# Moving the end of batch 14 to GpSimd, and x, bias and beta behind the last projection

## The chip, the cores and the metric

The kernel runs on one core of one Trainium2 chip. The metric is the device time of one execution in microseconds (us). Execution times of the same kernel are compared as medians of runs. The engines are named as in the profile: PE (TensorE, the matmuls), PEld (its weight loads), DVE (VectorE), ACT (ScalarE), POOL (GpSimd), SP (SyncE, which here only issues DMAs); "q" behind a name (SPq) is the sequencer that issues for that engine.

## The reference

One conditioned transformer attention layer on x of 16 batches x 256 tokens x 256 channels, 16 heads. The feed-forward weights W1 and W2 are passed in and not used.

```python
def _sln(h, w, ln_g, ln_b, Wg, bg, Wb, bb):
    mu = jnp.mean(h, axis=-1, keepdims=True)
    var = jnp.mean((h - mu) ** 2, axis=-1, keepdims=True)
    ln = (h - mu) / jnp.sqrt(var + EPS) * ln_g + ln_b
    gamma = (w @ Wg.T + bg)[:, None, :]
    beta = (w @ Wb.T + bb)[:, None, :]
    return gamma * ln + beta
...
h = _sln(hidden, w, ln_g, ln_b, Wg, bg, Wb, bb)
qkv = (h @ Wqkv.T + bqkv).reshape(B, N, num_heads, hd, 3)
...
energy = jnp.einsum('bhqd,bhkd->bhqk', q, k)
att = jax.nn.softmax(energy, axis=-1) / D ** 0.5
out = jnp.einsum('bhqk,bhkd->bhqd', att, v)
...
out = out @ Wp.T + bp
h1 = out + hidden
h2 = _sln(h1, w, ln_g, ln_b, Wg, bg, Wb, bb)
return h2 + h1
```

## The kernel before, in words

The kernel works through the 16 batches one after another, software-pipelined: while the scores, the exponentials and the weighing of batch b run, the maxima of batch b + 1, the projections of batch b + 2 and the first layer norm of batch b + 3 are made, and the second layer norm of batch b - 2 ends. Each engine has its own program, written out by hand in order; every dependence between engines is a wait on a semaphore, and an engine that waits holds all that stands behind it in its program. A batch's 256 tokens lie as two halves (t = 0, 1) of 128 partitions x 256 channels.

What the change touches is the tail behind the loop over the batches. There the last two batches are finished: batch 14 (B - 2) and batch 15 (B - 1).

The second layer norm of a batch has these steps, with a the batch (function `residual`, DVE): the residual h1 = m1 + x (stage 0, L784), its statistics (`bn_stats`, stage 1), mean and variance mv2 (`bn_aggr`, stage 2, after a short `memset` of `pause`), vare = variance + EPS (stage 3, L799), then y = (h1 - mean) * gamma (stage 4, L804, two instructions) and y = y * rstd + h1b (stage 5, L812, two instructions). POOL makes h1b = h1 + beta (`add_beta`, L396) and rstd = vare ** -0.5 (`rstd_out`, L403) between them. gamma and beta of a batch lie in `gb` (columns 0 to D, and D to 2D). vare, rstd, mv2, h1 and h1b of the second norm have a single buffer, y has two (batch parity). `ln2_step` counts the DVE steps of this norm, `rstd_ready` the powers on POOL, `y_ready` the finished batches.

In batch 15 the last half of the attention is projected twice by PE in `finish`: into the banks st0 and st1 (`project_half(k, 0)`, `projt_done`), where x and bias have been added by a matmul with the identity, for the statistics (L948) and for (h1 - mean) * gamma (L956); and into m1 (`project_half(k, 1)`, `projb_done`), where x, bias and beta are added in the same way. The sum x + bias + beta is made by POOL into the tile xn (L491, `xb2_ready`). Both wait for aT_l, the low half of the attention output turned round, which DVE makes in two pieces (`low_att_half`, L833) from what ACT evicted (L677). The last two DVE instructions (L963, `yt_ready`) make y = y * rstd + m1, one for each half.

SP issues the result transfers in this order: batch 14 whole, 256 KB, after `y_ready` reaches B - 1 (L348), then the two halves of batch 15, 128 KB each, after `yt_ready` (L351), and waits for all of them to land (L353).

Of the kernel before, what the change touches and what calls it, by code (L numbers as in the profile page):

```python
# [32 lines left out]
P = 128  # L33
# [24 lines left out]
def cond_block(nc, x, condT, vectors, WgT, WbT, WqkvT, WpT, bp, out):  # L58
    gb_dram = nc.dram_tensor("gb_rows", (B, 2 * D), F32, kind="Internal").ap()
    with ExitStack() as ctx:  # L60
# [165 lines left out]
        h1b_ready = sem("h1b_ready")  # L226
        y_ready = sem("y_ready")

        def wait(eng, s, value):
# [20 lines left out]
        def par(a):  # L250

            return a % 2
# [103 lines left out]
        def _(pool):  # L356
# [116 lines left out]
            for k in range(KT):  # L473
# [13 lines left out]
            add_beta(B - 2)  # L487
            rstd_out(B - 2)
            wait(pool, gb_in[par(B - 1)], 16 * (half(B - 1) + 1))
            wait(pool, xdb_ready, B)  # L490
            pool.tensor_tensor(xn[:], xbuf(B - 1), gb[:, par(B - 1), D:2 * D].rearrange("p (a n) -> p a n", a=1)  # L491
                               .broadcast_to([P, TT, D]), ALU.add).then_inc(xb2_ready, 1)
            rstd_out(B - 1)

# [185 lines left out]
        def _(dve):  # L680
# [261 lines left out]
            low_att_half(0)  # L942
            residual(B - 2, 4)
            low_att_half(1)
            residual(B - 2, 5)
            for t in range(TT):
                wait(dve, projt_done, t + 1)
                o = dve.bn_stats(stats2[:, t, :], st_ps[t][:, 0:D])  # L948
            o.then_inc(ln2_step, 1)
            residual(B - 1, 2)  # L950
            residual(B - 1, 3)
            a = B - 1
# [5 lines left out]
            o.then_inc(ln2_step, 1)  # L958
            wait(dve, ln2_step, 4 * a + 4)
            wait(dve, rstd_ready, 1 * a + 6)  # L960
# [6 lines left out]
        def _(pe):  # L967
# [237 lines left out]
            def project_half(k, into):  # L1205

                for t in range(TT):
                    l = (aT_h[:, k, t * P:(t + 1) * P], aT_l[:, k, t * P:(t + 1) * P])
                    ps = st_ps[t][:, 0:D] if into == 0 else m1[:, t * D:(t + 1) * D]
                    for n, (a, w) in enumerate(((l[0], wp_h), (l[1], wp_h), (l[0], wp_l))):  # L1210
                        o = mm(ps, a, w[:, k, :], False, k == KT - 1 and n == 2 and (into == 0 or t == TT - 1))
                    if k == KT - 1 and into == 0:
                        o.then_inc(projt_done, 1)
                if k == KT - 1 and into == 1:
                    o.then_inc(projb_done, 1)

            def finish():
# [20 lines left out]
                project_half(1, 0)  # L1238
                wait(pe, h1_ready, B - 1)
                pe.wait_ge(xb2_ready, 1)  # L1240
                for t in range(TT):
                    mm(m1[:, t * D:(t + 1) * D], ident[:], xn[:, t, :], t == 0, False)
                for k in range(KT):
                    project_half(k, 1)

# [131 lines left out]
```

## Time and profile before

| what | before |
|---|---|
| time, median of 3 runs | 350.76 us |
| the 3 runs | 350.86, 348.23, 350.76 us |
| the profiled execution, its own time | 349.5 us |
| its span, first to last instruction | 347.7 us |
| granted TensorE clock, mean over the span | 0.99 |
| PE busy | 334.0 us (96%) |
| PEld busy | 288.6 us (83%) |
| DVE busy | 297.0 us (85%) |
| ACT busy | 242.8 us (70%) |
| POOL busy | 159.0 us (46%) |
| chain that ended last, by engine | PE 86%, DVE 5%, ACT 2%, DMA 2%, POOL 2%, issue 2% |

The profile is one execution, and its own time is 1.8 us above its span. Busy time is the sum of an engine's instructions; the chain that ended last is followed back from the last instruction through what released each step. Times in the trace are counted from the start of the span, so the tail that the change touches lies between about 334 and 344 us.

### The profile page before, as it was taken

The page shows a single profiled execution, that of the slowest core. Times are in us where ns is not written, and L with a number is a line of the kernel's source. Part 1 is how long each engine was busy: PE and PEld are TensorE (multiplying, and loading weights), DVE is VectorE, ACT ScalarE, POOL GpSimd, SP SyncE. Part 2 cuts the span into 40 slices and gives each one's busy share as a digit, 9 for nine tenths or more (in the row PEclk, how much of TensorE's full clock was granted, in tenths as well). Part 3 has the DMA queues.
Part 4 walks back from the last instruction along what each step waited for, and adds up shares of the span by engine and source line. Part 5 has one row for each costly group of instructions (what it writes and reads, how often), then busy time and mean ns, then how long its engine had stood idle before and what let it go on. Part 6 is the DMA issues. An engine that isn't in the chain of part 4 may idle for free.

```text
span 347.7 us, 8982 instructions
## 1 busy us (share of the span) xinstructions
PE 334.0 (96%) x3173; PEld 288.6 (83%) x3173; DVE 297.0 (85%) x728; ACT 242.8 (70%) x476; POOL 159.0 (46%) x187
## 2 busy tenths in 40 slices
PE   8886989999999999999999999999999999999993
PEld 4675968889898888888898888888898888888773
DVE  4874877789898989989898989989898988998684
ACT  7762686868678686868687686868687686766740
POOL 5476261525464462726454462726454453225330
PEclk9997899999999999999999999999999999999999
DMA  8487245544555465565545565656546454652011
GB/s 239 128 202 204 58 123 151 150 134 129 161 131 158 135 180 155 136 173 139 157 133 156 134 176 153 141 154 160 156 135 154 106 170 124 168 147 75 18 60 60
DMA packets 47705, 48.87 MB, mean 141 GB/s; under 512 B 6287, under 2 KB 41374, under 8 KB 47662
## 3 DMA queue, kind: packets, MB, share of 16 engines
q1 hardware_dynamic: 44782, 47.00, 49.3%
q0 software_dynamic: 1984, 0.51, 0.9%
q10 hardware_dynamic: 896, 0.80, 0.8%
q8 instruction: 25, 0.41, 0.5%
q14 instruction: 18, 0.15, 0.1%
HBM read 9.99 MB, written 4.23 MB: 41 GB/s over the span
## 4 chain that ended last, share of the span: by engine, by line
PE 86%; DVE 5%; ACT 2%; DMA 2%; POOL 2%; issue 2%; SPq 0%; DVEq 0%; POOLq 0%; ACTq 0%
PE m L969 24%; PE st L969 19%; PE sa L969 18%; PE pv L969 17%; PE pv L1058 4%; PE pv L1139 2%; PE m L1098 2%; DMA wqkv<-WqkvT_dram 2%; DVE mx L688 1%; DVE qk_l L723 1%; POOL qk_l L415 1%; POOL xn L378 1%; PE pv L1072 1%; PE m L1072 1%; ACT qk_h L522 0%
## 5 line engine op out<-in xcount | busy, mean ns | idle before, releaser
L688 DVE TENSOR_REDUCE mx<-sa 128x2 f32<-128x512 f32 x256 | 171.6, 683 | 30.1 <-PE sa L969 29.0
L602 ACT ACTIVATE p<-st 128x512 f32<-128x512 f32 x240 | 140.9, 598 | 38.0 <-PE st L969 33.9
L969 PE MATMUL sa<-kst,qst 126*128 126x256 f32 x512 | 106.5, 290 | 1.6 <-DVE mx L688 1.1
L969 PE MATMUL st<-qst,kst 128*128 128x256 f32 x496 | 104.0, 292 | 0.7 <-DMA qst<-m_l 0.5
L969 PEld LDWEIGHTS st<-qst,kst 128*128 128x128 f32 x496 | 75.1, 188 | 14.3 <-issue 12.8
L969 PEld LDWEIGHTS sa<-kst,qst 126*128 126x128 f32 x512 | 80.0, 193 | 3.8 <-DVE mx L688 2.1
L369 POOL DMA_DIRECT2D qst<-m_h x31 | 17.6, 566 | 117.0 <-DVE m_l L697 117.0
L969 PE MATMUL pv<-p,v_st 128*32 128x256 f32 x1008 | 61.0, 382 | 0.0
L969 PEld LDWEIGHTS pv<-p,v_st 128*32 128x32 f32 x1008 | 29.5, 109 | 21.0 <-ACT p L602 1.8
L969 PE MATMUL m<-hT_h,wqkv_h 128*128 128x256 f32 x128 | 36.8, 300 | 1.4 <-issue 0.8
L378 POOL TENSOR_SCALAR xn<-xa,mv,rstd 128x256 f32<-128x256 f32 x28 | 34.2, 1227 | 1.4
L969 PE MATMUL m<-hT_h,wqkv_l 128*128 128x256 f32 x128 | 34.4, 280 | 0.4 <-DVE wqkv_l L909 0.4
L969 PE MATMUL m<-hT_l,wqkv_h 128*128 128x256 f32 x128 | 34.2, 279 | 0.0
L430 POOL TENSOR_TENSOR rstd<-vare,minus_half 128x4 f32<-128x4 f32 (+1 forms) x15 | 14.2, 947 | 40.4 <-DVE vare L745 36.3
L550 ACT ACTIVATE oT<-pv 128x512 f32<-128x512 f32 x29 | 17.2, 594 | 21.6 <-PE pv L969 21.6
L723 DVE SCALAR_TENSOR_TENSOR qk_l<-m,vecs,qk_h 128x256 fp32r<-128x256 f32 x60 | 25.9, 473 | 0.6 <-ACT qk_h L522 0.6
L969 PEld LDWEIGHTS m<-hT_h,wqkv_h 128*128 128x128 f32 x128 | 23.5, 189 | 2.3 <-ACT wqkv_h L642 1.2
L969 PEld LDWEIGHTS m<-hT_h,wqkv_l 128*128 128x128 f32 x128 | 23.6, 190 | 0.6 <-DVE wqkv_l L909 0.6
L969 PEld LDWEIGHTS m<-hT_l,wqkv_h 128*128 128x128 f32 x128 | 23.4, 187 | 0.0
L396 POOL TENSOR_TENSOR h1b<-h,gb 128x512 f32<-128x512 f32 x15 | 19.3, 1289 | 6.9 <-DVE h L784 6.9
L387 POOL TENSOR_TENSOR xa<-xa,bias_b 128x512 f32<-128x512 f32 x16 | 20.6, 1292 | 0.0
L410 POOL TENSOR_TENSOR hT_l<-hT,hT_h 128x512 fp32r<-128x512 f32 x14 | 18.0, 1289 | 4.0 <-ACT hT_h L503 4.0
(149 smaller groups left out, 568.3 us busy)
## 6 DMA issues: line engine op xcount, KB each, us to landing
qst<-qk_h SPq DMA_DIRECT2D x64, 128.0 KB, 2.4
qst<-qk_l SPq DMA_DIRECT2D x64, 128.0 KB, 2.5
kst<-qk_l SPq DMA_DIRECT2D x64, 128.0 KB, 2.7
kst<-qk_h SPq DMA_DIRECT2D x62, 128.0 KB, 2.4
xa<-x_dram SPq DMA_DIRECT2D x16, 256.0 KB, 3.0
gb<-gb_rows SPq DMA_DIRECT2D x16, 256.0 KB, 3.9
out_dram<-y SPq DMA_DIRECT2D x15, 256.0 KB, 3.4
wqkv<-WqkvT_dram SPq DMA_DIRECT2D x1, 512.0 KB, 5.8
```

The costliest lines, as they stand in the source:

```text
L369: pool.dma_start(raw(qst[MAX_ROW + r:MAX_ROW + 1 + r, p, g * HH:(g + 1) * HH, :]) .rearrange("a h (t n) -> a (h t) n", t=TT), raw(m[:, g, ...
L378: o = pool.tensor_scalar(xn[:, t, :], xbuf(a)[:, t, :], mv[:, t, 0:1], rstd[:, 0, t:t + 1], ALU.subtract, ALU.mult)
L387: pool.tensor_tensor(xbuf(a), xbuf(a), bias_b[:].rearrange("p (a n) -> p a n", a=1).broadcast_to([P, TT, D]), ALU.add).then_inc(xdb_ready, 1)
L396: pool.tensor_tensor(h1b[:], h1[:], gb[:, par(a), D:2 * D].rearrange("p (a n) -> p a n", a=1) .broadcast_to([P, TT, D]), ALU.add).then_inc ...
L410: pool.tensor_tensor(hT_l[:, par(a)], hT[:], hT_h[:, par(a)], ALU.subtract).then_inc(hTl_ready, 1)
L430: pool.tensor_tensor(rstd[:, which], vare[:, which], minus_half[:, which], ALU.pow).then_inc(rstd_ready, 1)
L550: nc.scalar.activation(oT[:, g, :], pv_ps[g][:], ACT.Copy).then_inc(oT_ready, 1)
L602: nc.scalar.activation(p32[:, h, :], st_ps[h % 2][:], ACT.Exp).then_inc(exp_done, 1)
L688: dve.tensor_reduce(mx[:, par(a), h // HH, (h % HH) * TT:(h % HH + 1) * TT], sa_ps[h % 2][:].rearrange("p (t n) -> p t n", t=TT), AX.X, AL ...
L723: o = dve.scalar_tensor_tensor(out=qk_l[:, par(a), t, g, :], in0=ps[:, g * N:(g + 1) * N], scalar=vecs[:, 4 + t, g:g + 1], in1=qk_h[:, par ...
L969: return nc.tensor.matmul(o, l, r, start=start, stop=stop)
L1058: o = nc.tensor.transpose(pv_ps[g][:, t * N + c * P:t * N + (c + 1) * P], oT[:, g, c * N + t * P:c * N + (t + 1) * P], ident[:])
```

## The change

Batch 14's last two steps leave DVE: the four instructions of stages 4 and 5 are gone from its program. POOL makes them in other pieces: right behind rstd of batch 14 two `tensor_scalar` make (h1 - mean) * rstd; then comes, as before, x + bias + beta for batch 15; then a `tensor_tensor` multiplies by gamma; then rstd of batch 15; then a `tensor_tensor` adds h1b and counts `y_ready`. A new semaphore `xhat_ready` orders these steps, and DVE waits until it is 2 before it overwrites mv2 with batch 15's values. The calls `residual(B - 1, 2)` and `residual(B - 1, 3)` are written out, since the count of `ln2_step` is one lower. On PE the two matmuls that add x, bias and beta into m1 stand behind the twelve of the projection instead of ahead of them. SP's program is the same.

```diff
--- before.py
+++ after.py
@@ -225,6 +225,7 @@
         ln2_step = sem("ln2_step")
         h1b_ready = sem("h1b_ready")
         y_ready = sem("y_ready")
+        xhat_ready = sem("xhat_ready")
 
         def wait(eng, s, value):
 
@@ -486,11 +487,24 @@
             add_beta(B - 3)
             add_beta(B - 2)
             rstd_out(B - 2)
+            a = B - 2
+            wait(pool, y_out[par(a)], 16 * half(a))
+            wait(pool, rstd_ready, 1 * a + 6)
+            for t in range(TT):
+                pool.tensor_scalar(y[:, par(a), t, :], h1[:, t, :], mv2[:, t, 0:1], rstd[:, 1, t:t + 1],
+                                   ALU.subtract, ALU.mult).then_inc(xhat_ready, 1)
             wait(pool, gb_in[par(B - 1)], 16 * (half(B - 1) + 1))
             wait(pool, xdb_ready, B)
             pool.tensor_tensor(xn[:], xbuf(B - 1), gb[:, par(B - 1), D:2 * D].rearrange("p (a n) -> p a n", a=1)
                                .broadcast_to([P, TT, D]), ALU.add).then_inc(xb2_ready, 1)
-            rstd_out(B - 1)
+            pool.wait_ge(xhat_ready, 2)
+            pool.tensor_tensor(y[:, par(a)], y[:, par(a)], gb[:, par(a), 0:D].rearrange("p (a n) -> p a n", a=1)
+                               .broadcast_to([P, TT, D]), ALU.mult).then_inc(xhat_ready, 1)
+            wait(pool, ln2_step, 4 * (B - 1) + 2)
+            pool.tensor_tensor(rstd[:, 1], vare[:, 1], minus_half[:, 1], ALU.pow).then_inc(rstd_ready, 1)
+            wait(pool, h1b_ready, B - 1)
+            pool.wait_ge(xhat_ready, 3)
+            pool.tensor_tensor(y[:, par(a)], y[:, par(a)], h1b[:], ALU.add).then_inc(y_ready, 1)
 
         @block.scalar
         def _(act):
@@ -940,15 +954,19 @@
             normalise_half(0)
             normalise_half(1)
             low_att_half(0)
-            residual(B - 2, 4)
             low_att_half(1)
-            residual(B - 2, 5)
             for t in range(TT):
                 wait(dve, projt_done, t + 1)
                 o = dve.bn_stats(stats2[:, t, :], st_ps[t][:, 0:D])
             o.then_inc(ln2_step, 1)
-            residual(B - 1, 2)
-            residual(B - 1, 3)
+            dve.wait_ge(xhat_ready, 2)
+            wait(dve, ln2_step, 4 * (B - 1))
+            dve.memset(pause[:], 0.0)
+            for t in range(TT):
+                o = dve.bn_aggr(mv2[:, t, :], stats2[:, t, :])
+            o.then_inc(ln2_step, 1)
+            wait(dve, ln2_step, 4 * (B - 1) + 1)
+            dve.tensor_scalar(vare[:, 1], mv2[:, :, 1], EPS, None, ALU.add).then_inc(ln2_step, 1)
             a = B - 1
             wait(dve, y_out[par(a)], 16 * half(a))
             wait(dve, gb_in[par(a)], 16 * (half(a) + 1))
@@ -956,7 +974,7 @@
                 o = dve.scalar_tensor_tensor(out=y[:, par(a), t, :], in0=st_ps[t][:, 0:D], scalar=mv2[:, t, 0:1],
                                              in1=gb[:, par(a), 0:D], op0=ALU.subtract, op1=ALU.mult)
             o.then_inc(ln2_step, 1)
-            wait(dve, ln2_step, 4 * a + 4)
+            wait(dve, ln2_step, 4 * a + 3)
             wait(dve, rstd_ready, 1 * a + 6)
             dve.wait_ge(projb_done, 1)
             for t in range(TT):
@@ -1208,11 +1226,10 @@
                     l = (aT_h[:, k, t * P:(t + 1) * P], aT_l[:, k, t * P:(t + 1) * P])
                     ps = st_ps[t][:, 0:D] if into == 0 else m1[:, t * D:(t + 1) * D]
                     for n, (a, w) in enumerate(((l[0], wp_h), (l[1], wp_h), (l[0], wp_l))):
-                        o = mm(ps, a, w[:, k, :], False, k == KT - 1 and n == 2 and (into == 0 or t == TT - 1))
+                        o = mm(ps, a, w[:, k, :], into == 1 and k == 0 and t == 0 and n == 0,
+                               into == 0 and k == KT - 1 and n == 2)
                     if k == KT - 1 and into == 0:
                         o.then_inc(projt_done, 1)
-                if k == KT - 1 and into == 1:
-                    o.then_inc(projb_done, 1)
 
             def finish():
                 wait(pe, att_ready, 2 * B - 1)
@@ -1237,11 +1254,12 @@
                 pe.wait_ge(aTtl_ready, 2)
                 project_half(1, 0)
                 wait(pe, h1_ready, B - 1)
+                for k in range(KT):
+                    project_half(k, 1)
                 pe.wait_ge(xb2_ready, 1)
                 for t in range(TT):
-                    mm(m1[:, t * D:(t + 1) * D], ident[:], xn[:, t, :], t == 0, False)
-                for k in range(KT):
-                    project_half(k, 1)
+                    o = mm(m1[:, t * D:(t + 1) * D], ident[:], xn[:, t, :], False, t == TT - 1)
+                o.then_inc(projb_done, 1)
 
             def step(b):
                 for h in range(H):
```

The end of DVE's program before, from the last normalise of the attention's second half. A row is a line, an operation and what it writes from what; `sa`, `pv`, `st` and `m` are banks of PSUM, `h` is h1, `mv` is mv2, `stats` is stats2:

```order
L833 TENSOR_TENSOR aT_l<-sa,aT_h 128x256 [waits aTth_ready]
L804 SCALAR_TENSOR_TENSOR y<-h,mv,gb 128x256 [waits gb_in0,y_out0]
L804 SCALAR_TENSOR_TENSOR y<-h,mv,gb 128x256
L833 TENSOR_TENSOR aT_l<-pv,aT_h 128x256 [waits aTth_ready]
L812 SCALAR_TENSOR_TENSOR y<-y,rstd,h1b 128x256 [waits h1b_ready,rstd_ready,ln2_step]
L812 SCALAR_TENSOR_TENSOR y<-y,rstd,h1b 128x256
L948 BN_STATS stats<-st 128x6 [waits projt_done] x2
L793 MEMSET pause 128x1 [waits ln2_step]
L795 BN_AGGR mv<-stats 128x2 x2
L799 TENSOR_SCALAR vare<-mv 128x2 [waits ln2_step]
```

The same place of the changed kernel (its lines are 14 to 18 higher):

```order
L847 TENSOR_TENSOR aT_l<-sa,aT_h 128x256 [waits aTth_ready]
L847 TENSOR_TENSOR aT_l<-pv,aT_h 128x256 [waits aTth_ready]
L960 BN_STATS stats<-st 128x6 [waits projt_done] x2
L964 MEMSET pause 128x1 [waits ln2_step,xhat_ready]
L966 BN_AGGR mv<-stats 128x2 x2
L969 TENSOR_SCALAR vare<-mv 128x2 [waits ln2_step]
L974 SCALAR_TENSOR_TENSOR y<-st,mv,gb 128x256 [waits gb_in1,y_out1]
L974 SCALAR_TENSOR_TENSOR y<-st,mv,gb 128x256
L981 SCALAR_TENSOR_TENSOR y<-y,rstd,m 128x256 [waits projb_done,rstd_ready,ln2_step]
```

The two pairs of batch 14 are out; the two halves of aT_l stand next to each other, and the `memset` has a second wait. What follows `vare` is as before.

The end of POOL's program before:

```order
L396 TENSOR_TENSOR h1b<-h,gb 128x512 [waits y_ready,h1_ready,gb_in0]
L403 TENSOR_TENSOR rstd<-vare,minus_half 128x2 [waits y_ready,ln2_step]
L491 TENSOR_TENSOR xn<-xa,gb 128x512 [waits xdb_ready,gb_in1]
L403 TENSOR_TENSOR rstd<-vare,minus_half 128x2 [waits y_ready,ln2_step]
```

And of the changed kernel:

```order
L397 TENSOR_TENSOR h1b<-h,gb 128x512 [waits y_ready,h1_ready,gb_in0]
L404 TENSOR_TENSOR rstd<-vare,minus_half 128x2 [waits y_ready,ln2_step]
L494 TENSOR_SCALAR y<-h,mv,rstd 128x256 [waits rstd_ready,y_out0]
L494 TENSOR_SCALAR y<-h,mv,rstd 128x256
L498 TENSOR_TENSOR xn<-xa,gb 128x512 [waits xdb_ready,gb_in1]
L501 TENSOR_TENSOR y<-y,gb 128x512 [waits xhat_ready]
L504 TENSOR_TENSOR rstd<-vare,minus_half 128x2 [waits ln2_step]
L507 TENSOR_TENSOR y<-y,h1b 128x512 [waits xhat_ready,h1b_ready]
```

Two instructions now stand ahead of the one that makes xn, one more ahead of rstd of batch 15, and one behind it, which releases batch 14's transfer.

## Rows read from the trace of the kernel before

**Rows 1.** The chain that ended last, its end: start us, us, what.

```profile
337.80 0.41 DVE aT_l L833
338.22 0.68 DVE y L804 x2
338.89 0.22 issue
339.12 0.42 DVE aT_l L833
339.58 0.97 PE st L969 x6
340.56 2.24 PE m L969 x16
...
342.92 0.48 DVE y L963
```

**Rows 2.** Timeline of ACT: start us, us, engine, line, operation, [idle before].

```profile
338.41 0.38 ACT L677 ACTIVATE aT_h<-pv 128x256 fp32r<-128x256 f32 x1 [1.33 <-PE pv L1233]
```

**Rows 3.** Timeline of PE, the last of st, the identity matmuls, the last of m.

```profile
340.28 0.28 PE L969 MATMUL st<-wp_l,aT_h 128*128 128x256 f32 x1
340.39 1.03 PE L969 MATMUL m<-xn,ident 128*128 128x256 f32 x4
...
342.51 0.28 PE L969 MATMUL m<-wp_l,aT_h 128*128 128x256 f32 x1
```

**Rows 4.** Timeline of DVE in the tail.

```profile
340.24 0.79 DVE L948 BATCH_NORM_STATS2 stats<-st 128x6 f32<-128x256 f32 x2
...
341.35 0.17 DVE L799 TENSOR_SCALAR vare<-mv 128x2 f32<-128x2 f32 x1
341.43 0.88 DVE L956 SCALAR_TENSOR_TENSOR y<-st,mv,gb 128x256 f32<-128x256 f32 x2
342.92 0.87 DVE L963 SCALAR_TENSOR_TENSOR y<-y,rstd,m 128x256 f32<-128x256 f32 x2 [0.62 <-PE m L969]
```

**Rows 5.** Timeline of POOL in the tail.

```profile
334.85 1.29 POOL L396 TENSOR_TENSOR h1b<-h,gb 128x512 f32<-128x512 f32 x1 [6.89 <-DVE h L784]
336.57 0.71 POOL L403 TENSOR_TENSOR rstd<-vare,minus_half 128x2 f32<-128x2 f32 x1 [0.43 <-DVE vare L799]
337.24 1.27 POOL L491 TENSOR_TENSOR xn<-xa,gb 128x512 f32<-128x512 f32 x1
341.59 0.71 POOL L403 TENSOR_TENSOR rstd<-vare,minus_half 128x2 f32<-128x2 f32 x1 [3.08 <-DVE vare L799]
```

**Rows 6.** Timeline of SP's transfers, of batch 14 and of batch 15.

```profile
340.34 0.34 SPq L348 DMA_DIRECT2D out_dram<-y  x1
343.43 0.81 SPq L351 DMA_DIRECT2D out_dram<-y  x2
```

**Rows 7.** Instructions on tile y from 338 to 346 us, and SP's last wait.

```profile
L804 DVE SCALAR_TENSOR_TENSOR y<-h,mv,gb x2: 473/568/664, 338.1 to 338.7; 128x256 f32<-128x256 f32 x2
L351 SPq DMA_DIRECT2D out_dram<-y x2: 337/380/422, 343.4 to 343.8; - x2
DMA to landing us min/median/max: 1.7/1.8/2.0
...
L353 SPq EVENT_SEMAPHORE  x1: 17/17/17, 345.6 to 345.6; - x1
```

**Rows 8.** Groups of POOL instructions, each shape apart: count | busy us, mean ns | idle.

```profile
L378 POOL TENSOR_SCALAR xn<-xa,mv,rstd 128x256 f32<-128x256 f32 x28 | 34.2, 1227 | 1.4
L387 POOL TENSOR_TENSOR xa<-xa,bias_b 128x512 f32<-128x512 f32 x16 | 20.6, 1292 | 0.0
...
L474 POOL TENSOR_SCALAR bias_cols<-ones,vecs 128x128 f32<-128x128 f32 x2 | 0.7, 369 | 0.2
```

**Rows 9.** Line L378 alone: duration ns min/median/max.

```profile
L378 POOL TENSOR_SCALAR xn<-xa,mv,rstd x28: 1209/1228/1232, 26.4 to 277.1; 128x256 f32<-128x256 f32 x28
```

**Rows 10.** Timeline of POOL in the loop: a power, then the tensor_scalar pair.

```profile
79.71 1.03 POOL L430 TENSOR_TENSOR rstd<-vare,minus_half 128x4 f32<-128x4 f32 x1 [2.98 <-DVE vare L745]
80.85 2.44 POOL L378 TENSOR_SCALAR xn<-xa,mv,rstd 128x256 f32<-128x256 f32 x2
```

**Rows 11.** Line L745 in two stretches, and POOL beside its second start.

```profile
L745 DVE TENSOR_SCALAR vare<-mv x1: 168/168/168, 4.6 to 4.6; 128x2 f32<-128x2 f32 x1
...
L745 DVE TENSOR_SCALAR vare<-mv x2: 169/363/557, 13.0 to 17.2; 128x2 f32<-128x2 f32 x2
...
16.24 3.81 POOL L458 MEMSET kst<- 128x512 f32 x8 [2.22 <-DVE xn L750]
```

**Rows 12.** Groups of DVE instructions: the add that POOL's is compared with.

```profile
L784 DVE TENSOR_TENSOR h<-m,xa 128x512 f32<-128x512 f32 x15 | 10.1, 671 | 1.0 <-PE m L969 1.0
```

**Rows 13.** Transfers between 325 and 348 us: GB/s in 40 slices.

```profile
GB/s 0 10 19 0 0 0 0 0 28 0 0 0 0 0 0 221 310 157 75 146 4 0 0 0 0 0 0 0 324 132 0 0 0 157 276 23 0 0 0 0
```

## The prediction, on record before the changed kernel ran

> **What bounds the kernel now.** Over its whole span PE is the bound, but nothing that the change touches lies ahead of 337 us, so I read only the end. I went to the chain that ended last, from its end backwards [rows 1]: the last DVE instruction waits for PE's projection into m1, PE's projection waits for the second aT_l of DVE (339.12), and that aT_l stood behind two y instructions of batch 14 (338.22, 0.68 us). The timeline of ACT [rows 2] shows what that place cost: ACT had finished the input of that aT_l at 338.41 + 0.38 = 338.79, and DVE began at 339.12. So 0.3 us of the chain is DVE's work for batch 14, sitting in the way of batch 15. Behind it the chain is PE alone until 342.79 [rows 3], then L963 at 342.92 [rows 4], then two issues of SP from 343.43 to 344.24, SP's wait until the landing at 345.6, and the close of the program [rows 6, 7].
>
> Two things in these views matter as much as the chain. POOL idles 3.08 us ahead of the rstd of batch 15 [rows 5]: that is the room the change wants to fill. And SP issues batch 14 at 340.34, right after DVE's L812, 3.1 us ahead of the first half of batch 15 [rows 6]: today the order "14, then 15" on SP's queue costs nothing, because 14 is long done.
>
> **The change part by part.**
>
> *DVE loses four instructions.* The second aT_l can start at 338.79 + 0.04 (the step between two engines in the chain is 0.02 to 0.05 us) = 338.83 in place of 339.12: 0.3 us earlier. PE's six matmuls into st then start at 339.28 instead of 339.58, the second bn_stats follows 0.3 us earlier too, since it began at 340.60, just behind PE's last st matmul (340.28 + 0.28 = 340.56) [rows 3, 4]; so vare of batch 15 moves from 341.35 to 341.05, and L956's pair from 341.43 to 341.13. The new wait of the memset for xhat_ready = 2 asks for 339.8 (below) and is met a microsecond ahead.
>
> *PE's order.* The same twelve matmuls into m1 and the same two identity matmuls (four records, 1.03 us) in another order: no cost by itself. What it buys is cover: xn is needed at 341.5 in place of 340.1. Before, from the start of st to the end of m PE took 342.79 - 339.58 = 3.21 us; now it ends at 339.28 + 3.21 = 342.5, if xn is there when PE has done the twelve, at about 341.5. Had the order stayed, PE would have waited for xn until 341.0.
>
> *POOL gains four instructions.* I follow its queue by start times, with its own rows for each kind. Neighbouring POOL instructions overlap by 0.04 us (336.57 + 0.71 against 337.24) [rows 5]; one that waits for the one before it starts 0.1 us after its end (79.71 + 1.03 = 80.74 against 80.85) [rows 10].
> - rstd of batch 14 ends at 336.57 + 0.71 = 337.28, unchanged.
> - Two tensor_scalar with two per-partition scalars, 128x256: the same form as L378, 28 times in the trace, 1.209 to 1.232 us each with DVE busy beside it [rows 9]; 2.43 us a pair, from 337.38 to 339.81.
> - xn, 1.27 us [rows 5]: from 339.77 to 341.04. PE has it 0.4 us before it wants it.
> - The multiply by gamma, 128x512 from two SBUF tiles. No multiply of this form is in the trace. Nearest is the add of the same shape, 1.27 to 1.29 us [rows 5, 8]. Bounds: not below 0.74 (two of L474's 0.369 for 128 columns, which does two operations but reads one tensor [rows 8]), not above the 2.45 of two L378. I take the add, since only the operation differs: 341.00 to 342.29.
> - rstd of batch 15: now 342.25 to 342.96, where before it ran 341.59 to 342.30. DVE's last pair waits for it and can start at 343.00 instead of 342.92. The whole gain of the first step is eaten here, and 0.08 us more.
> - The add of h1b, 1.29 us [rows 5]: 342.92 to 344.21. Only this counts y_ready.
>
> *SP's queue.* Here the end is set. Batch 14's transfer stands ahead of batch 15's on SP, and it is now released at 344.21, not at 340.31. It issues at 344.24, takes 0.34 us and a gap of 0.04, and the two halves follow in 0.81 us: the last issue ends at 344.24 + 0.38 + 0.81 = 345.43, where it ended at 344.24 [rows 6]. That is **+1.2 us**. The rows of batch 15, ready at 343.48 and 343.87, wait for nothing but SP's order.
>
> *The transfers themselves.* 512 KB now leave in one piece where 256 KB did. Landing took 2.0 us for the whole batch and 1.7 to 1.8 for a half [rows 7]. Unhindered the last half lands 1.8 us behind its issue at 345.02, at 346.82. If instead it queues: batch 14 lands at 346.24, and the other 256 KB at the best rate of a slice, 324 GB/s [rows 13], take 0.8 us more: 347.05. So 0 to +0.25 us; I take +0.1, since a half takes nearly as long to land as a whole (1.8 against 2.0), so size is the small part of it.
>
> Sum: 1.2 + 0.1 = **+1.3 us** on the profiled execution: span 347.7 + 1.3 = 349.0, time 349.5 + 1.3 = 350.8.
>
> The profiled 349.5 lies inside the three runs (348.23, 350.76, 350.86), whose median is 350.76. With the median as base the sum gives 352.1, with the profiled run 350.8. These runs lie wider apart than the effect, so I take a value between: **351.5 us**.
>
> A row and a rule on moving elementwise work. An add of 128x512 takes DVE 0.671 us [rows 12] and POOL 1.29 [rows 8], a ratio of 1.92; and the new POOL work is 2.45 + 1.29 + 1.29 = 5.0 us against the 0.87 x 2 DVE spends. The Trainium skill, GPSIMD Engine Reference, section 3.1, has POOL 1.96 times slower at an add of 2048 fp32 elements and says that "use DVE for elementwise" stays the rule. The trace agrees on the ratio for an add; by the rule's ratio alone the moved 1.74 us would be 3.4 us and POOL would be done 1.6 us sooner, at 342.6, so the rule's direction is right and its size too kind for this form.
>
> **The rivals.**
>
> *A. vare held up by POOL.* vare of batch 15 wants to start at 341.05, 0.05 us after POOL's multiply. The trace shows a DVE instruction of this very form held: L745 took 0.557 us at 17.2 in place of 0.168, while POOL ran back-to-back memsets of 0.48 us [rows 11]; and the first L804 took 0.664 in place of 0.473, begun while POOL's xn was running [rows 5, 7]. If vare is held to the end of the multiply, it ends at about 342.35, the power starts at 342.4 instead of 342.25, and all behind it is 0.15 us later; L974's pair ends at 343.25, DVE's last pair at 344.1, still ahead of SP. Total +1.45: 352.9 on the median base, 351.65 by my middle value. Against it: the start times are equal within their error, so vare may slip in first.
> The Trainium skill, SBUF — State Buffer, section "Who interferes with whom", says that a DVE instruction in a 2-port mode (tensor_scalar can be one) and a POOL instruction exclude each other for a whole instruction. Both rows above agree that DVE is held; by it rival A would be the rule whenever the multiply starts first.
>
> *B. The multiply is dear.* At its upper bound, 2.45, rstd of batch 15 and the last add move 1.16 us: +2.5 in all, 352.7. For it: no multiply row; against it: its neighbours differ by 0.02.
>
> *C. Hidden or faster.* POOL's chain ends early enough that SP issues 14 before 15 is ready. Then PE's 0.3 us gain shows: -0.3, 349.9. It needs y_ready by about 342.6, that is 1.6 us off the 5.0 of new POOL work. If the two tensor_scalar cost as L474 does (0.74 each) it saves only 1.0: y_ready 343.23, last issue ends 343.26 + 0.38 + 0.81 = 344.45, +0.2. The 28 rows of L378 speak against even that.
>
> *D. Slower by over 1%.* POOL's new instructions stretched because both engines work on the same memory in turn. To pass 3.5 us, the 5.0 us must grow by 3.5 - 1.3 = 2.2 us, 44%; at twice the length it is +5.0 + 1.3 = +6.3, 357. Against it: L378's 28 durations lie within 2% beside a busy DVE [rows 9], and DVE's instructions here mostly read PSUM.
>
> **How the numbers follow.** Forecast as summed (POOL's chain and SP's order, +1.0 to +1.35): 0.47. A: 0.30. B: 0.12. C: 0.07. D: 0.04. All but D lie within 1%, about what a measurement of this kernel can tell from no change (350.76 +/- 3.5). Chances: faster by over 1% 0.01, within 1% 0.95, slower by over 1% 0.04. Range: below, the forecast on the lowest run, 348.23 + 1.3 = 349.5, and C just under it; above, B on the median base, 350.76 + 2.5 = 353.3. I give 349.2 to 353.3.
>
> **What would show each step.** In the profile after: the second aT_l on DVE near 338.85 and PE's first st matmul 0.3 us sooner than before; POOL without a gap from 336.6 to 344.2, with 1.23 us for each new tensor_scalar and 1.29 for the multiply; rstd of batch 15 near 342.3, released not by DVE but by POOL's own queue; DVE's last pair waiting for rstd, not for PE; batch 14's transfer issued near 344.2 with both halves of batch 15 right behind it, and the last landing near 346.9. A is shown by vare of over 1 us. I am wrong if SP's three issues don't stand together at the end, or if y_ready falls before 343.

## The result, and the profile after

| what | before | changed |
|---|---|---|
| time, median (22 runs each) | 349.01 us (348.04 to 351.09) | 351.16 us (350.26 to 352.94) |
| ratio to before, 95% interval | | 1.0055 (1.0038 to 1.0072) |
| the profiled execution, its own time | 349.5 us | 351.13 us |
| its span | 347.7 us | 349.3 us |

The changed kernel is slower by 0.55%, 1.9 us (1.3 to 2.5), within the 1% called no change in the prediction but clear of zero; the two medians lie 2.15 us apart. One of the 12 executions of a_no_mul, below, was a slow one of 817 us, and its ratio leaves it out. In the page the busy times show little: POOL has 4 instructions and 6.3 us more (159.0 to 165.3), DVE 4 instructions less.

```profile
span 349.3 us, 8981 instructions
PE 334.0 (96%) x3173; PEld 288.6 (83%) x3173; DVE 296.6 (85%) x724; ACT 242.5 (69%) x476; POOL 165.3 (47%) x191
```

The tail of the changed kernel, timeline of POOL (start us, us, engine, line, operation), which answers to [rows 5]:

```profile
336.06 0.71 POOL L404 TENSOR_TENSOR rstd<-vare,minus_half 128x2 f32<-128x2 f32 x1 [0.44 <-DVE vare L813]
336.95 2.44 POOL L494 TENSOR_SCALAR y<-h,mv,rstd 128x256 f32<-128x256 f32 x2 [0.18 <-POOL rstd L404]
339.36 1.30 POOL L498 TENSOR_TENSOR xn<-xa,gb 128x512 f32<-128x512 f32 x1
340.62 1.28 POOL L501 TENSOR_TENSOR y<-y,gb 128x512 f32<-128x512 f32 x1
341.99 0.72 POOL L504 TENSOR_TENSOR rstd<-vare,minus_half 128x2 f32<-128x2 f32 x1
342.68 1.27 POOL L507 TENSOR_TENSOR y<-y,h1b 128x512 f32<-128x512 f32 x1
```

Timeline of DVE, which answers to [rows 4]:

```profile
338.33 0.42 DVE L847 TENSOR_TENSOR aT_l<-pv,aT_h 128x256 fp32r<-128x256 f32 x1 [0.61 <-ACT aT_h L691]
339.47 0.78 DVE L960 BATCH_NORM_STATS2 stats<-st 128x6 f32<-128x256 f32 x2 [0.71 <-PE st L987]
...
340.67 1.24 DVE L969 TENSOR_SCALAR vare<-mv 128x2 f32<-128x2 f32 x1
341.83 0.86 DVE L974 SCALAR_TENSOR_TENSOR y<-st,mv,gb 128x256 f32<-128x256 f32 x2
342.80 0.87 DVE L981 SCALAR_TENSOR_TENSOR y<-y,rstd,m 128x256 f32<-128x256 f32 x2
```

Timeline of PE (its last rows) and of SP, which answer to [rows 3] and [rows 6]:

```profile
341.03 1.03 PE L987 MATMUL m<-xn,ident 128*128 128x256 f32 x4
...
343.97 0.34 SPq L349 DMA_DIRECT2D out_dram<-y  x1
344.35 0.93 SPq L352 DMA_DIRECT2D out_dram<-y  x2
```

The span starts of two executions are no good origin: the tail of this one began 0.5 us sooner than before's (rstd of batch 14 on POOL at 336.06 against 336.57 [rows 5]), in parts of the program that are alike. From here on, "at x" without more is counted in us from the start of that instruction, which nothing in any of these kernels touches. In this measure, before: POOL's last instruction ends at 5.73, SP's last issue at 7.67, the span at 11.13. Changed: 7.89, 9.22 and 13.24. So the tail is **2.1 us** longer, and the span shows 1.6 only because of the 0.5 ahead of it. The span and the rows of the programs' close are printed to 0.1 us, so sums that use them are good to about 0.05.

2.1 us is more than SP's issues are late (1.55) and more than the last landing is late: SP passes its last wait (taken here and below as the start of its first closing row, the COMPARE_BRANCH of line L60, whose rows follow under a_no_mul) at 9.13 before and at 10.74 after, 1.6. What lies between that wait and the end grew from 2.0 to 2.5 us, with nothing in the change that would explain it. That rest is what the experiments followed.

### The profile page after: what moved, and what is told of

Its sections match the earlier page's. It is cut to its first block, busy times and chain, and to the rows that moved or that the text cites. A ratio compares the mean times of both kernels' runs of the same rounds, so it can differ in the third digit from the quotient of the medians.

```text
span 349.3 us, 8981 instructions
## 1 busy us (share of the span) xinstructions
PE 334.0 (96%) x3173; PEld 288.6 (83%) x3173; DVE 296.6 (85%) x724; ACT 242.5 (69%) x476; POOL 165.3 (47%) x191
## 4 chain that ended last, share of the span: by engine, by line
PE 84%; DVE 5%; ACT 4%; POOL 3%; issue 2%; POOLq 0%; ACTq 0%; DVEq 0%
PE m L987 23%; PE st L987 18%; PE sa L987 18%; PE pv L987 17%; PE pv L1076 4%; PE pv L1157 2%; PE m L1116 2%; DVE mx L702 1%; ACT qst L620 1%; DVE qk_l L737 1%; POOL qk_l L416 1%; POOL xn L379 1%; PE pv L1090 1%; PE m L1090 1%; ACT qk_h L536 0%
```

## The experiments

Theory 1 is the prediction's: POOL's chain releases batch 14's transfer late, SP's order holds batch 15 behind it, and the last landing sets the end. The first four kernels test it.

**b_hold14**, before with batch 14's transfer held back until the first half of batch 15 is ready, so that SP's three issues stand together as in the changed kernel, and no compute touched:

```diff
+            sp.wait_ge(yt_ready, 1)
             wait(sp, y_ready, B - 1)
             sp.dma_start(out_t[B - 2], y[:, par(B - 2)]).then_inc(y_out[par(B - 2)], 16)
```

> The kernel before, with one wait more on SP: batch 14's transfer is issued only when the first half of batch 15 is ready (as in the changed kernel it stands directly ahead of the two halves); no compute engine is touched. Times counted from the start of the rstd of batch 14 on POOL: before, SP's last issue ends at 7.67 us, its last wait at 9.03, the span at 11.1; in the changed kernel 9.22, 10.74, 13.2. Theory 1 (SP's order and three transfers close together are a cost of their own): last issue ends at 8.05 (+0.38), last wait at 9.6 (+0.55), and if the longer close of the program (2.5 us in place of 2.1) comes from the three transfers too, the span ends at 12.1, +1.0; with a close of 2.1 it is +0.55. Rival (only POOL's chain costs, the transfers overlap freely): last wait +0.38 and close 2.1, +0.4 in all.

Measured: ratio to before 0.9997 (0.9973 to 1.0021). Its span is 347.6 us, and rstd of batch 14 starts at 336.50. Rows of SP and of the close:

```profile
343.74 0.93 SPq L352 DMA_DIRECT2D out_dram<-y  x2
...
L60 POOLq DRAIN  x1: 5892/5892/5892, 341.5 to 341.5; - x1
L60 SPq COMPARE_BRANCH  x1: 33/33/33, 346.2 to 346.2; - x1
```

SP's last issue ends at 8.17 (+0.5), its last wait at 9.70 (+0.57), as theory 1 said, and the span ends at 11.10: not a trace of it arrived at the end. Both theories on record were wrong here; the close shrank by what the landing was late, so the end hangs on something else.

**a_15first**, the changed kernel with batch 15's halves issued first:

```diff
-            wait(sp, y_ready, B - 1)
-            sp.dma_start(out_t[B - 2], y[:, par(B - 2)]).then_inc(y_out[par(B - 2)], 16)
             for t in range(TT):
                 sp.wait_ge(yt_ready, t + 1)
                 sp.dma_start(out_t[B - 1][:, t, :], y[:, par(B - 1), t, :]).then_inc(y_out[par(B - 1)], 16)
+            wait(sp, y_ready, B - 1)
+            sp.dma_start(out_t[B - 2], y[:, par(B - 2)]).then_inc(y_out[par(B - 2)], 16)
```

> The changed kernel with SP's last issues turned round: the two halves of batch 15 first, batch 14 behind them. Theory 1 (batch 14 ahead on SP's queue holds batch 15 back): the halves issue at 7.2 us from the start of rstd of batch 14 and end by 8.15, batch 14 issues at 8.2, last issue ends at 8.55 in place of 9.22, last landing at about 10.2 in place of 10.74; 0.5 to 0.7 us faster than the changed kernel, still 1.0 to 1.5 us slower than before. Rival (POOL's late end is all of it, order is nothing): no faster than the changed kernel.

Measured: 1.0049 (1.0029 to 1.0070). Its span is 349.0 us, and rstd of batch 14 starts at 335.69:

```profile
342.94 0.81 SPq L350 DMA_DIRECT2D out_dram<-y  x2
343.80 0.45 SPq L352 DMA_DIRECT2D out_dram<-y  x1
...
L60 SPq COMPARE_BRANCH  x1: 33/33/33, 346.0 to 346.0; - x1
```

SP's last issue ends at 8.56, its last wait at 10.31, both 0.4 to 0.7 sooner than in the changed kernel, and the span ends at 13.31 against 13.24. Again what SP gains is not seen.

**a_act_vare**, the changed kernel with vare of batch 15 made by ACT (`eps_col` is a column holding EPS):

```diff
+            wait(act, ln2_step, 4 * (B - 1) + 1)
+            nc.scalar.activation(vare[:, 1], mv2[:, :, 1], ACT.Identity, bias=eps_col[:]).then_inc(vare_act, 1)
...
-            dve.tensor_scalar(vare[:, 1], mv2[:, :, 1], EPS, None, ALU.add).then_inc(ln2_step, 1)
...
-            wait(pool, ln2_step, 4 * (B - 1) + 2)
+            pool.wait_ge(vare_act, 1)
```

> The changed kernel, but variance + EPS of batch 15 is made by ACT, which is idle there, in place of DVE. Theory (rival A of the prediction: vare, 1.24 us in place of 0.16, was held by POOL's multiply): ACT's instruction takes under 0.4 us although POOL's multiply runs, the subtract and multiply by gamma on DVE start 1.1 us earlier, POOL's power starts right behind its multiply, 0.13 us sooner (5.80 us from the start of rstd of batch 14 in place of 5.93), and all behind it the same 0.13. Rival (vare was late for another reason, such as the wait on xhat_ready): ACT's instruction is as late or as long.

Measured: 1.0078 (1.0050 to 1.0105), too wide to tell 0.16 us: it holds the changed kernel's 1.0055, and lies above it if anywhere. What follows is read from the traces alone. Its timelines of ACT, POOL and DVE:

```profile
341.28 0.30 ACT L697 ACTIVATE vare<-mv,eps_col 128x2 f32<-128x2 f32 x1 [2.43 <-DVE mv L973]
...
341.15 1.29 POOL L504 TENSOR_TENSOR y<-y,gb 128x512 f32<-128x512 f32 x1
342.39 0.72 POOL L507 TENSOR_TENSOR rstd<-vare,minus_half 128x2 f32<-128x2 f32 x1
...
341.22 0.88 DVE L980 SCALAR_TENSOR_TENSOR y<-st,mv,gb 128x256 f32<-128x256 f32 x2
```

ACT's instruction takes 0.30 us in the middle of POOL's multiply; on DVE the same addition of EPS, with the same multiply beside it, took 1.24 and ended at 340.67 + 1.24 = 341.91, the end of the multiply (340.62 + 1.28 = 341.90). The power starts at 5.77 in place of 5.93, and the end comes at 13.08 in place of 13.24. Rival A is shown in the traces, one of each kernel, with its price: 0.16 us.

**a_no_mul**, the changed kernel without POOL's multiply by gamma for batch 14, which is left out of the computation:

```diff
-            pool.wait_ge(xhat_ready, 2)
-            pool.tensor_tensor(y[:, par(a)], y[:, par(a)], gb[:, par(a), 0:D].rearrange("p (a n) -> p a n", a=1)
-                               .broadcast_to([P, TT, D]), ALU.mult).then_inc(xhat_ready, 1)
...
-            pool.wait_ge(xhat_ready, 3)
+            pool.wait_ge(xhat_ready, 2)
```

> The changed kernel without POOL's multiply by gamma for batch 14 (that part of the computation is left out). Theory (POOL's queue sets the end, SP's order passes it on): xn's add is followed by the power as soon as vare is there, vare takes 0.16 again, the add of h1b ends 1.1 us sooner, batch 14 issues at about 6.8 us from the start of rstd of batch 14 in place of 7.91, the last issue ends at 8.1 in place of 9.22: 1.1 us faster. Rival (PE or DVE bound the end by then): under 0.5 us faster.

Measured: 1.0027 (1.0002 to 1.0052); vare 0.17 us, SP's last issue at 8.14, the end at 12.22, 1.0 sooner than in the changed kernel. POOL's last instruction ends at 6.81, 1.08 sooner. SP moved by as much here, so this kernel alone doesn't part the two; but together with b_hold14 and a_15first it is the clue: the end follows POOL, whether SP moves or not. In the six traces at hand the span ends 5.35 to 5.42 us behind POOL's last instruction. The rows of line L60, where each engine's program closes, say why. Before and changed (start us behind the durations in ns):

```profile
L60 POOLq DRAIN  x1: 5892/5892/5892, 341.6 to 341.6; - x1
L60 DVEq DRAIN  x1: 853/853/853, 343.0 to 343.0; - x1
L60 SPq COMPARE_BRANCH  x1: 33/33/33, 345.7 to 345.7; - x1
L60 POOLq EVENT_SEMAPHORE  x2: 17/17/17, 347.5 to 347.6; - x2
L60 SPq EVENT_SEMAPHORE  x1: 17/17/17, 347.6 to 347.6; - x1
```

```profile
L60 POOLq DRAIN  x1: 7056/7056/7056, 342.0 to 342.0; - x1
L60 DVEq DRAIN  x1: 853/853/853, 342.9 to 342.9; - x1
L60 SPq COMPARE_BRANCH  x1: 33/33/33, 346.8 to 346.8; - x1
L60 POOLq EVENT_SEMAPHORE  x2: 17/17/17, 349.1 to 349.2; - x2
L60 SPq EVENT_SEMAPHORE  x1: 17/17/17, 349.3 to 349.3; - x1
```

POOL's queue closes with a DRAIN that ends at 341.6 + 5.9 = 347.5 before and at 342.0 + 7.1 = 349.1 in the changed kernel, 5.2 us behind POOL's last instruction in both, and all other engines pass their last semaphore right behind it. SP is through its wait for the landing 1.8 to 2.3 us earlier and only waits for POOL. The row of a DRAIN can start before the engine's last instruction, so what counts is where it ends: DVE's ends at 343.0 + 0.85, less than 0.1 us behind DVE's last instruction (343.79). This is **theory 2**: POOL's last instruction plus 5.4 us ends the program, unless SP's last wait, plus 0.4, is later.

**b_pool_late**, before with an add on POOL whose result is not used:

```diff
             rstd_out(B - 1)
+            pool.wait_ge(rstd_ready, B + 5)
+            pool.tensor_tensor(h1b[:], h1[:], gb[:, par(B - 2), D:2 * D].rearrange("p (a n) -> p a n", a=1)
+                               .broadcast_to([P, TT, D]), ALU.add)
```

> The kernel before with one add of 128x512 more on POOL behind its last power; nothing waits for it and its result is not used. The profiles so far show a DRAIN on POOL's queue that ends 5.2 us behind POOL's last instruction, and the span ends 0.2 us behind that: 5.35 to 5.4 us behind POOL's last instruction in each of six kernels. Theory 2 (that DRAIN ends the program): POOL's last instruction ends 7.0 us from the start of rstd of batch 14 in place of 5.7, the span ends at 12.4 in place of 11.1, +1.25 us, although SP's last wait stays at 9.0. Theory 1 (SP's transfers end it): no change.

Measured: 1.0065 (1.0039 to 1.0091). The timelines of POOL and SP, and the close:

```profile
341.90 1.27 POOL L495 TENSOR_TENSOR h1b<-h,gb 128x512 f32<-128x512 f32 x1
...
342.95 0.81 SPq L351 DMA_DIRECT2D out_dram<-y  x2
...
L353 SPq EVENT_SEMAPHORE  x1: 17/17/17, 345.2 to 345.2; - x1
...
L60 POOLq DRAIN  x1: 6436/6436/6436, 341.9 to 341.9; - x1
```

SP's last issue ends at 7.68 and its wait at 9.12, as before to 0.01 us, and the span ends at 12.42 in place of 11.13: +1.29, for an instruction that nobody waits for. Theory 1 gives nothing here. The ratio says more, 2.3 us (1.4 to 3.2): it bears out that the kernel is slower, the size of 1.29 is the trace's, and what lies between the two is not explained.

**b_act_root**, before with batch 15's 1/sqrt off POOL. The power on POOL goes; ACT and DVE have in its place:

```diff
+            nc.scalar.activation(spare[:], eps_col[:], ACT.Sqrt)
+            wait(act, ln2_step, 4 * (B - 1) + 2)
+            nc.scalar.activation(vare[:, 1], mv2[:, :, 1], ACT.Sqrt, bias=eps_col[:]).then_inc(root_ready, 1)
...
-            residual(B - 1, 3)
...
+            dve.wait_ge(root_ready, 1)
+            dve.reciprocal(rstd[:, 1], vare[:, 1]).then_inc(ln2_step, 1)
...
-            rstd_out(B - 1)
```

> The kernel before with batch 15's 1/sqrt(variance + EPS) off POOL: ACT makes the square root (with a first use of the function ahead of time, so that its table is there), DVE the reciprocal of 128x2. POOL's last instruction is then the add that makes xn, ending 1.95 us from the start of rstd of batch 14 in place of 5.7. Theory 2: POOL's DRAIN ends by 7.2, so SP's last wait at 9.0 sets the end, and the span ends at 9.4 in place of 11.1: 1.7 us faster than before. Theory 1 (SP's transfers and a fixed close of 2.1 us behind them): no change, 11.1.

Measured: 0.9957 (0.9933 to 0.9982), 1.5 us faster than before (0.6 to 2.3). Rows of its ACT, of SP and of its close:

```profile
340.17 1.28 ACT L682 ACT_TABLE_LOAD   x1
341.46 0.20 ACT L682 ACTIVATE spare<-eps_col 128x1 f32<-128x1 f32 x1
342.70 0.30 ACT L684 ACTIVATE vare<-mv,eps_col 128x2 f32<-128x2 f32 x1 [1.03 <-DVE mv L802]
...
344.81 0.81 SPq L355 DMA_DIRECT2D out_dram<-y  x2
...
L60 POOLq DRAIN  x1: 6819/6819/6819, 338.2 to 338.2; - x1
...
L60 SPq COMPARE_BRANCH  x1: 33/33/33, 347.1 to 347.1; - x1
```

POOL's DRAIN is over at 345.0, 2.1 us ahead of SP's wait, which now sets the end: 9.58, 1.55 sooner than before, although batch 15's results are issued no sooner (7.70). Faster than both kernels.

**b_best**, the same with two edits more:

```diff
-            residual(B - 2, 4)
-            low_att_half(1)
...
+            for t in range(TT):
+                o = dve.scalar_tensor_tensor(out=y[:, par(a), t, :], in0=h1[:, t, :], scalar=mv2[:, t, 0:1],
+                                             in1=gb[:, par(a), 0:D], op0=ALU.subtract, op1=ALU.mult)
+                if t == 0:
+                    low_att_half(1)
...
+            act.wait_ge(yt_ready, 2)
+            act.dma_start(out_t[B - 1][:, 1, :], y[:, par(B - 1), 1, :]).then_inc(y_out[par(B - 1)], 16)
```

> b_act_root, and two edits more: the second aT_l of DVE stands between the two halves of batch 14's subtract and multiply in place of behind both, and the second half of batch 15's result is issued by ACT's queue beside SP's. Theory 2: PE's last projections start 0.25 us sooner, the two halves issue at once (0.4 us), and with POOL's DRAIN long over both show: the span ends at 8.7 us from the start of rstd of batch 14, 2.4 us faster than before. Under theory 1 it would be 0.65 faster.

Measured: 0.9918 (0.9890 to 0.9946), median 346.75 us, 2.9 us faster than before by the ratio (1.9 to 3.8). In the trace the end is at 9.25, 1.9 sooner than before and 0.3 sooner than in b_act_root; 8.7 was expected. Timelines of SP, ACT and DVE:

```profile
342.17 0.34 SPq L354 DMA_DIRECT2D out_dram<-y  x1
...
342.57 0.38 ACTq L685 DMA_DIRECT2D out_dram<-y  x1
...
341.66 0.87 DVE L980 SCALAR_TENSOR_TENSOR y<-y,rstd,m 128x256 f32<-128x256 f32 x2 [0.18 <-PE m L986]
```

The 0.24 us of PE arrived (DVE's last pair at 6.11 in place of 6.35 [rows 4, 5]), but the second queue brought next to nothing: the second half is ready only at 342.53, when SP would have been free again. I had counted 0.4 us of issue time that lies behind DVE's own work.

The other four isolate parts of the change. **a_pe_old**, the changed kernel with PE's old order:

```diff
+                pe.wait_ge(xb2_ready, 1)
+                for t in range(TT):
+                    mm(m1[:, t * D:(t + 1) * D], ident[:], xn[:, t, :], t == 0, False)
                 for k in range(KT):
                     project_half(k, 1)
-                pe.wait_ge(xb2_ready, 1)
-                for t in range(TT):
-                    o = mm(m1[:, t * D:(t + 1) * D], ident[:], xn[:, t, :], False, t == TT - 1)
-                o.then_inc(projb_done, 1)
```

> The changed kernel with PE's old order: the identity matmuls that add x, bias and beta stand ahead of the twelve of the last projection. PE then waits for xn until 4.6 us from the start of rstd of batch 14, its projection ends 0.4 us later than in the changed kernel, and DVE's last pair starts at 7.15 in place of 6.74. POOL's last instruction stays at 7.9, so by theory 2 the end stays at 13.2; by theory 1 too, since batch 14's issue at 7.9 still goes first.

One execution. PE waits for xn, and DVE's last pair starts at 7.35, 0.6 later than in the changed kernel (0.4 expected), yet the end is at 13.24, the same:

```profile
341.66 1.10 PE L987 MATMUL m<-xn,ident 128*128 128x256 f32 x4 [0.98 <-POOL xn L498]
```

**b_pe_new**, before with the new order on PE alone (the same lines the other way round):

> The kernel before with the change's order on PE alone: x, bias and beta are added into m1 behind the twelve matmuls of the last projection. xn is there 2 us before either order wants it. PE's last projection ends where it did, within 0.1 us, and the span ends at 11.1 us from the start of rstd of batch 14, under both theories.

One execution: DVE's last pair at 6.42 in place of 6.35, the end at 11.12. By itself PE's reordering makes DVE's last pair 0.07 us later and moves the end by nothing; in the changed kernel it hides what POOL's xn is late.

**b_split**, before with the second aT_l between the two halves of batch 14's subtract and multiply (the first part of b_best's edit, alone):

> The kernel before with the second aT_l of DVE between the two halves of batch 14's subtract and multiply; nothing else. PE's last projection and DVE's last pair come 0.25 us sooner, SP's last wait at 8.8 us from the start of rstd of batch 14 in place of 9.05. Theory 2: the power on POOL stays where it was within 0.05 us, so the span ends at 11.1 as before: a step on the chain that the profile names is shortened and the end does not move. Theory 1: the end moves 0.25 us.

One execution: PE and DVE's last pair 0.27 sooner, SP's last wait at 8.84 (9.13 before), and the end at 11.34, 0.2 **later**. It was expected unchanged. The reason is in theory 2's own measure: POOL's power ends at 5.94 in place of 5.73, since vare comes later. Its rows of DVE (rstd of batch 14 starts at 335.26):

```profile
337.86 0.48 DVE L947 SCALAR_TENSOR_TENSOR y<-h,mv,gb 128x256 f32<-128x256 f32 x1
338.38 0.88 DVE L812 SCALAR_TENSOR_TENSOR y<-y,rstd,h1b 128x256 f32<-128x256 f32 x2
339.17 0.76 DVE L955 BATCH_NORM_STATS2 stats<-st 128x6 f32<-128x256 f32 x2
```

The same instructions stand ahead of bn_stats, but L812 now comes directly behind the instruction whose count it waits for, and starts 0.04 us after that one's end, where before the aT_l lay between and the starts overlapped; and the aT_l is started only when ACT is done. bn_stats starts at 3.91 in place of 3.67. The chain that the profile printed for before got shorter and the program longer.

**a_h1b_dve**, the changed kernel with the add of h1b given back to DVE:

```diff
-            wait(pool, h1b_ready, B - 1)
-            pool.wait_ge(xhat_ready, 3)
-            pool.tensor_tensor(y[:, par(a)], y[:, par(a)], h1b[:], ALU.add).then_inc(y_ready, 1)
...
+            wait(dve, h1b_ready, B - 1)
+            dve.wait_ge(xhat_ready, 3)
+            dve.tensor_tensor(y[:, par(B - 2)], y[:, par(B - 2)], h1b[:], ALU.add).then_inc(y_ready, 1)
```

> The changed kernel with its last POOL instruction, the add of h1b for batch 14, given back to DVE, ahead of DVE's last pair. Theory 2 (POOL's last instruction sets the end): POOL's last instruction is the power, ending 6.65 us from the start of rstd of batch 14 in place of 7.89; the span ends at 12.0 to 12.05 in place of 13.24, 1.2 us faster than the changed kernel and still 0.9 slower than before, although DVE's last pair starts 0.5 us later and its results with it. Theory 1: SP's last issue ends at 8.65 in place of 9.22, 0.6 faster than the changed kernel.

Measured: 1.0023 (0.9990 to 1.0055); DVE's last pair starts at 7.14, 0.4 later than in the changed kernel, POOL's last instruction ends at 6.64, and the end is at 12.06: 1.2 sooner. Its close:

```profile
L60 POOLq DRAIN  x1: 5902/5902/5902, 343.9 to 343.9; - x1
L60 SPq COMPARE_BRANCH  x1: 33/33/33, 348.1 to 348.1; - x1
```

All of them side by side. The first column is where rstd of batch 14 starts in the trace; the others are in us from there (worked out from the timelines, the L60 rows and the spans; the last column is the end less POOL's last end):

| kernel | rstd of batch 14 starts | POOL's last instruction ends | SP's last wait over | span ends | behind POOL |
|---|---|---|---|---|---|
| before | 336.57 | 5.73 | 9.13 | 11.13 | 5.40 |
| b_pe_new | 335.38 | 5.74 | 9.22 | 11.12 | 5.38 |
| b_hold14 | 336.50 | 5.73 | 9.70 | 11.10 | 5.37 |
| b_split | 335.26 | 5.94 | 8.84 | 11.34 | 5.40 |
| a_h1b_dve | 338.04 | 6.64 | 10.06 | 12.06 | 5.42 |
| a_no_mul | 337.78 | 6.81 | 9.72 | 12.22 | 5.41 |
| b_pool_late | 336.08 | 7.09 | 9.12 | 12.42 | 5.33 |
| a_act_vare | 336.62 | 7.73 | 10.58 | 13.08 | 5.35 |
| a_pe_old | 336.96 | 7.86 | 10.74 | 13.24 | 5.38 |
| changed | 336.06 | 7.89 | 10.74 | 13.24 | 5.35 |
| a_15first | 335.69 | 7.89 | 10.31 | 13.31 | 5.42 |
| b_act_root | 337.92 | 1.95 | 9.18 | 9.58 | 7.63 |
| b_best | 335.55 | 1.95 | 8.85 | 9.25 | 7.30 |

In eleven kernels the end is 5.33 to 5.42 behind POOL, whatever SP does between 8.84 and 10.74; in the two where POOL is done early it is 0.40 behind SP's last wait. The scatter of 0.1 us is no more than the rounding of the spans. The ratios of the changed kernel, a_15first, a_act_vare, a_no_mul, b_pool_late, b_act_root and b_best are clear of 1 on the side that the table has; that of a_h1b_dve holds 1. The order among the slower kernels is the traces' alone, one of each, and b_split, b_pe_new and a_pe_old were executed only once.

## Why the prediction was right in its number and wrong in its reason

- **DVE's gain**: right. The second aT_l starts 0.04 behind ACT (337.91 + 0.38, then 338.33), at 2.27 in place of 2.55, 0.28 sooner for the 0.29 forecast. vare started only 0.17 sooner (4.61 in place of 4.78), not 0.30: the memset, which now has two waits, began 0.14 behind bn_stats in place of 0.06. It cost nothing, since POOL's multiply was running anyway.
- **PE's order and cover**: right. xn was there (its add ends at 340.66) before PE's identity matmuls at 341.03; the order alone costs PE 0.07 us and is worth nothing at the end (b_pe_new).
- **POOL's queue**: right in its rows and nearly in its sum. The pair took 2.44 (2.43 forecast), the multiply 1.28 (1.29), the last add 1.27. The wait of POOL on itself ahead of the pair was 0.18, not 0.10, and with rival A's 0.16 the last instruction ended at 7.89 where the forecast's 344.21 is 7.64. Bound B was far off: a multiply costs what an add costs.
- **Rival A**: came true, at 0.16 us for the 0.15 worked out. The Trainium skill, SBUF — State Buffer, section "Who interferes with whom", has the loser blocked for the other's whole instruction; the trace agrees, vare ending at 341.91 and the multiply at 341.90, and a_act_vare frees the power from it. In which mode the DVE instruction ran, on which the Trainium skill makes it depend there, no run here shows.
- **SP's queue, "here the end is set"**: this is the step that failed. Its own numbers were near (the last issue ended 1.55 later, 1.2 forecast), but b_hold14 and a_15first show that neither the issues nor the landings carried anything to the end. The last landing before is at 345.6 [rows 7] and the span ends at 347.7: I wrote off these 2.1 us as "the close of the program" without asking what ran in them. It was POOL's DRAIN, which ends 5.2 us behind POOL's last instruction: that instruction sets the end (b_pool_late, b_act_root). The chain that the profile prints for before stops at DVE's close, whose last row ends at 343.79, 3.9 us short of the end, which should have told me the same. The signs that I had named ahead (three issues together, batch 14's near 344.2, the last landing near 346.9, vare over 1 us) came, at 343.97 and 346.8, but none of them could part SP's end from POOL's.
- **The size**: with the right mechanism and the forecast's own rows the sum would have been 344.21 - 342.30 = 1.91 us, the whole delay of POOL's last instruction [rows 5]. With rival A and the longer self-wait it is 7.89 - 5.73 = 2.16, and the tail's 13.24 - 11.13 = 2.11 is that, within the rounding. I forecast 1.3; measured were 1.9 (1.3 to 2.5) by the ratio.
- **The number**: 351.5 against 351.16 came out close by luck, because two errors met. The medians lie 2.15 us apart, 0.85 more than the sum, and the base between the profiled run and the three runs' median (350.2) stood 1.2 us above the median of 22 runs, 349.01; 0.34 is left. Rival A's sum on the median base is also wrong in itself: 350.76 + 1.45 is 352.2, not 352.9; no bound rests on it.
- **Rival C** had the right question (does y_ready come before 342.6) for the wrong engine: it is not when batch 14 is issued that counts, but when POOL is done. Its gain of 0.3 us from PE would not have shown either: b_split had it, and its end came 0.2 later. The rule that the Trainium skill, GPSIMD Engine Reference, section 3.1, gives, that elementwise work belongs on DVE, spoke against the change, and the traces agree: POOL took 2.44 + 1.28 + 1.27 = 4.99 us for what DVE had done in 1.06 and 0.86.

## What to carry to other kernels

Before costing a change in the tail, find what ends the program: compare the end of the printed chain and the last landing with the end of the span, and look at the closing rows of each engine. If one engine's close is long, as POOL's 5.2 us here, its last instruction's end is what counts, even if nobody waits for that instruction; so let that engine finish first and put late work on the others. Two executions are compared from a common instruction near the change, since everything ahead of it moves by more (here 335.3 to 338.0 us for the same instruction) than the change is worth.

## What the runs showed of the hardware that was not expected

- GpSimd's queue closes with a DRAIN that ends 5.11 to 5.19 us behind its last instruction in all 13 kernels, after a power or an add, and whether its last DMA was issued 13 us before that instruction's end (b_act_root), 17 (before) or 19 (changed). DVE's DRAIN ends less than 0.1 us behind DVE's last instruction, and ACT's no more than 0.2 behind its own. What the 5.2 us are made of was not tried: every kernel here issues DMAs from GpSimd, so whether they cause it stays open.
- A DVE tensor_scalar of 128x2 elements, 0.16 to 0.17 us alone, took 1.20 to 1.25 us in each kernel where GpSimd's 128x512 multiply ran beside it; ACT's took 0.30 there.
- Three result transfers issued together landed hardly later for it: batch 14's took 2.0 us from issue to landing in both kernels, and the halves of batch 15 1.9 to 2.0 in the changed kernel against 1.7 to 1.8 before.
